# Weight scan with four load slots instead of two, and the first activation ladder on the vector engine alone: a two-layer Mamba and BitNet block on eight cores

## The reference, cut to what matters

```python
def act_quant(x):                     # per token, 8 bits
    scale = 127.0 / jnp.clip(jnp.max(jnp.abs(x), axis=-1, keepdims=True), EPS)
    return jnp.clip(jnp.round(x * scale), -128.0, 127.0) / scale
def weight_quant(w):                  # one scale for the whole matrix
    scale = jnp.clip(jnp.mean(jnp.abs(w)), EPS)
    return jnp.clip(jnp.round(w / scale), -1.0, 1.0) * scale
def h_bitlinear(x, w):
    return einsum(act_quant(fwht(x)), weight_quant(w))      # fwht: Hadamard rotation
x = x + mamba_and_ffn(layernorm(x))
y = layernorm(x)
x = x + h_bitlinear(silu(h_bitlinear(y, w_gate)) * h_bitlinear(y, w_up), w_down)
```

## Time and profile before

| what | value |
|---|---|
| median of three timed runs | 9508.48 us |
| lowest and highest of the three | 9263.67 and 9608.37 us |
| the profiled execution's own time | 9270.68 us |
| span of its slowest core (core 0) | 9269.1 us |
| spans of the eight cores | 9202.2 to 9269.1 us |
| granted TensorE clock, mean of each core | 0.767 to 0.769 |
| vector engine busy | 4310.0 us (46%) |
| TensorE matmuls busy | 4426.5 us (48%) |
| data moved by DMA on that core | 724.60 MB |

### The profile page before, as it was taken

The page is one execution under the profiler, slowest core; times in us unless marked ns, Lnnn a source line. Parts: engine busy times, 40 slices in busy tenths (PEclk is TensorE's granted clock), DMA queues, the critical chain, the costliest instruction groups (busy, mean ns, idle before and its releaser), DMA issues.

```text
span 9269.1 us, 76271 instructions; the slowest of 8 cores (9202.2 to 9269.1 us)
## 1 busy us (share of the span) xinstructions
PE 4426.5 (48%) x19532; PEld 1986.7 (21%) x19854; DVE 4310.0 (46%) x5807; ACT 1545.5 (17%) x2319; POOL 863.9 (9%) x859
## 2 busy tenths in 40 slices
PE   0002324854444365889889550688873000322247
PEld 0000111332332122334334120233330000110112
DVE  2222532443333331000000268677777888666678
ACT  2222231211101210000000013111110333121210
POOL 0000000000000000000000013100000343222210
PEclk9999657965555688999999775899985555666679
DMA  7764213310000033333333100344431000222247
GB/s 252 254 246 157 58 21 78 59 17 4 4 3 4 0 73 82 60 61 70 61 60 68 50 1 0 120 145 148 146 120 50 28 0 3 80 62 82 62 124 217
DMA packets 208574, 724.60 MB, mean 78 GB/s; under 512 B 49137, under 2 KB 50066, under 8 KB 179474
## 3 DMA queue, kind: packets, MB, share of 16 engines
q1 hardware_dynamic: 81890, 361.01, 11.7%
q0 software_dynamic: 68336, 205.28, 11.2%
q10 hardware_dynamic: 57920, 153.40, 5.4%
HBM read 817.63 MB, written 33.55 MB: 92 GB/s over the span
## 4 chain that ended last, share of the span: by engine, by line
PE 34%; DVE 33%; ACT 8%; DMA 8%; issue 8%; POOLq 5%; DVEq 3%; ACTq 2%; SPq 0%
PE pb L1087 10%; PE pb L1526 5%; PE pb L1132 5%; POOLq L85 5%; DVE arena L1199 4%; PE pb L365 3%; DVE arena L1696 3%; DVE arena L1210 2%; DVE arena L1405 2%; ACT arena L1187 2%; DMA arena<-fdT 2%; DMA arena<-fuT 2%; DMA arena<-fgT 2%; PE pb L789 2%; DVE arena L1692 2%
## 5 line engine op out<-in xcount | busy, mean ns | idle before, releaser
L1087 PE MATMUL pb<-arena 128*128 128x512 bf16 x4014 | 906.0, 381 | 330.3 <-DVE arena L1099 208.2
L1526 PE MATMUL pb<-arena 128*128 128x512 bf16 x4014 | 899.8, 380 | 119.5 <-DVE arena L1564 103.1
L1187 ACT ACTIVATE arena<-arena,c_ladthr 128x512 f32<-128x512 f32 x800 | 577.4, 722 | 2021.1 <-POOL arena L1222 1975.2
L1199 DVE SCALAR_TENSOR_TENSOR arena<-arena 128x512 f32<-128x512 f32 x800 | 705.7, 882 | 371.2 <-ACT arena L1187 306.1
L1222 POOL TENSOR_TENSOR arena<-arena 128x512 f32<-128x512 f32 x480 | 660.0, 1375 | 2088.5 <-DVE arena L1210 2032.9
L365 PE MATMUL pb<-arena 128*128 128x512 bf16 (+1 forms) x2853 | 506.8, 328 | 216.3 <-DMA arena<-winT 139.0
L1784 PE MATMUL pb<-arena 128*128 128x512 bf16 x2004 | 502.7, 405 | 202.6 <-DVE arena L1696 119.0
L1099 DVE TENSOR_TENSOR arena<-arena,pb 128x512 bf16<-128x512 bf16 x128 | 87.9, 687 | 1059.7 <-ACT arena L1094 1059.7
L1087 PEld LDWEIGHTS pb<-arena 128*128 128x128 bf16 x4096 | 393.3, 98 | 844.1 <-issue 394.6
L1526 PEld LDWEIGHTS pb<-arena 128*128 128x128 bf16 x4096 | 393.0, 98 | 627.3 <-issue 172.6
L1405 DVE TENSOR_REDUCE arena<-arena 128x1 f32<-128x2048 f32 x96 | 219.5, 2286 | 588.1 <-DMA arena<-fgT 197.3
(11 more groups left out here) (206 smaller groups left out, 5370.6 us busy)
## 6 DMA issues: line engine op xcount, KB each, us to landing
arena<-fdT ACTq DMA_DIRECT2D x256, 512.0 KB, 4.6
arena<-fgT SPq DMA_DIRECT2D x64, 1024.0 KB, 5.7
arena<-fuT SPq DMA_DIRECT2D x64, 1024.0 KB, 6.1
arena<-fdT SPq DMA_DIRECT2D x64, 1024.0 KB, 6.2
arena<-fgT SPq DMA_DIRECT2D x128, 512.0 KB, 4.2
arena<-fuT POOLq DMA_DIRECT2D x128, 512.0 KB, 4.2
arena<-wgT POOLq DMA_DIRECT2D x64, 512.0 KB, 5.0
arena<-wuT POOLq DMA_DIRECT2D x64, 512.0 KB, 5.0
```

Source lines behind the costliest of these rows:

```text
L1087: e.matmul(p[:, 0:nns], w[:, jj * 128:(jj + 1) * 128], self.rms2[:, jj * T + nn0:jj * T + nn0 + nns], start=st, stop=sp),
L1187: e.activation(cc[:], ss[:], AF.Sign, bias=self.ladthr[:, 16 + jj:17 + jj]),
L1199: e.scalar_tensor_tensor(ww[:], cc[:], -0.5 * kk, ss[:], OP.mult, OP.add),
L1526: e.matmul(pp[:, 0:nns], t2[:, jj * 128:(jj + 1) * 128], xq[:, jj * T + nn0:jj * T + nn0 + nns], start=st, stop=sp),
```

## The change

Three edits. In p0 the scan gets four slots instead of two: four buffers of 128 x 2048 float32, four semaphores (`p0x0` to `p0x3`), four loads ahead, and the load of tile j+4 is issued behind the sum of tile j. The split of the sums over the two engines stays. In p5 the ladder is no longer `ladder2_pair` on four tiles of 512 columns but `ladder` on one tile of 128 x 1024 after another, entirely on the vector engine. And `ln2` stays allocated until the end of p5 instead of being freed before the ladder; this alone issues no instruction and removes no barrier.

```diff
     def p5(self, stk, sC, sXQ):
-        sLN2 = ExitStack()
-        ln2 = self.sb(sLN2, [128, 16 * T], BF16, "ln2")
+        ln2 = self.sb(stk, [128, 16 * T], BF16, "ln2")
...
         Ss.barrier()
-        sLN2.close()
...
-        lbufs = [tuple(self.sb(stk, [128, 512], F32) for _ in range(3))
-                 for _ in range(4)]
-        for c in range(0, 16, 2):
-            tiles = [(c, 0), (c, 1), (c + 1, 0), (c + 1, 1)]
-            self.ladder2_pair(
...
-                lbufs, [("v", 0)] * 4)
+        v0 = self.sb(stk, [128, T], F32)
+        vt = self.sb(stk, [128, T], F32)
+        ct = self.sb(stk, [128, T], F32)
+        for c in range(16):
+            self.ladder(Y1[:, c * T:(c + 1) * T], scbc[:, 0:T], 0, T,
+                        xq[:, c * T:(c + 1) * T], v0, vt, ct, from_psum=False)
         Ss.barrier()

     def p0(self, stk):
-        wt_ = [self.sb(stk, [128, 2048], F32) for _ in range(2)]
+        wt_ = [self.sb(stk, [128, 2048], F32) for _ in range(4)]
...
-        st2 = Stream2(self, "sync", "p0x")
-        st2.load(0, wt_[0][:], srcs[0])
-        st2.load(1, wt_[1][:], srcs[1])
-        vprev, aprev = 0, 0
+        st2 = Stream2(self, "sync", "p0x", nslots=4)
+        for s4 in range(4):
+            st2.load(s4, wt_[s4][:], srcs[s4])
         for j, src in enumerate(srcs):
             if j % 2 == 0:
-                st2.wait("scalar", 0)
+                st2.wait("scalar", j % 4)
...
             else:
-                st2.wait("vector", 1)
+                st2.wait("vector", j % 4)
...
-            if j + 2 < len(srcs):
-                st2.load(j % 2, wt_[j % 2][:], srcs[j + 2],
-                         guard=(("a", aprev) if j % 2 == 0 else ("v", vprev)))
+            if j + 4 < len(srcs):
+                st2.load(j % 4, wt_[j % 4][:], srcs[j + 4], guard=tok)
```

More of the change, by code:

```diff
@@ L1391, in p0 @@
                 srcs.append(self.hbm["fdT"][m, :, q4 * 2048:(q4 + 1) * 2048])
-        st2 = Stream2(self, "sync", "p0x")
-        st2.load(0, wt_[0][:], srcs[0])
-        st2.load(1, wt_[1][:], srcs[1])
-        vprev, aprev = 0, 0
+        st2 = Stream2(self, "sync", "p0x", nslots=4)
+        for s4 in range(4):
+            st2.load(s4, wt_[s4][:], srcs[s4])
         for j, src in enumerate(srcs):
             if j % 2 == 0:
-                st2.wait("scalar", 0)
-                aprev = Ss.emit("scalar", lambda e, b=wt_[j % 2], jj=j:
-                                e.activation(dummy[:], b[:], AF.Abs,
-                                             accum_out=col[:, jj:jj + 1]), inc="a")
-            else:
-                st2.wait("vector", 1)
[L1404 to L1407, removed]
-            if j + 2 < len(srcs):
-                st2.load(j % 2, wt_[j % 2][:], srcs[j + 2],
-                         guard=(("a", aprev) if j % 2 == 0 else ("v", vprev)))
+                st2.wait("scalar", j % 4)
+                tok = ("a", Ss.emit(
+                    "scalar", lambda e, b=wt_[j % 4], jj=j:
+                    e.activation(dummy[:], b[:], AF.Abs,
+                                 accum_out=col[:, jj:jj + 1]), inc="a"))
+            else:
+                st2.wait("vector", j % 4)
+                tok = ("v", Ss.emit(
+                    "vector", lambda e, b=wt_[j % 4], jj=j:
+                    e.reduce_sum(col[:, jj:jj + 1], b[:],
+                                 axis=mybir.AxisListType.X,
+                                 apply_absolute_value=True), inc="v"))
+            if j + 4 < len(srcs):
+                st2.load(j % 4, wt_[j % 4][:], srcs[j + 4], guard=tok)
         Ss.barrier()
```

## The result

| | before | after |
|---|---|---|
| profiled execution | 9270.68 us | 9087.77 us |
| median of ten timed runs | 9458.35 us | 9201.34 us |
| lowest and highest | 9263.67 and 9672.41 us | 9081.15 and 9504.13 us |
| ratio of the two kernels' comparable runs | | 0.9818, 95% interval 0.9748 to 0.9889 |

The kernel became faster, by 1.1 to 2.5%; whether by more than 2% is not settled by these runs. Predicted were 9065 us (8980 to 9270) against the profiled execution, 2.2% less.

The account below looks back on a forecast made before the run. The prediction took p0 to be bound by the turn of its two load slots, and the ladder by a chain over three engines. It summed 9270.7 - 217 - 5 + 7 = 9056, said 9065 us, range 8980 to 9270.

Parts of the forecast that it names:

- The bound of p0: In p0, the turn of a slot (8.30 us, two side by side) limits the scan; more outstanding loads fill the missing 0.28.
- The rate: In p0 with four slots, DMA was taken to deliver 348 GB/s, so p0 takes 585.5 us, a gain of 217 us.
- if the time of a packet stays as it is: In p0, the assumption that scales a share of 0.73 at 256 GB/s to 351 GB/s at full share.
- the first rival: In p0, packets get longer with all cores asking; at 300 GB/s gain 125 us, kernel 9148 us; chance 0.28.
- the short stretches of 401 and 430: Full DMA stretches in p0, read as bounds from above; at 401 GB/s gain 293 us, kernel 8980 us, chance 0.10.
- those of 218 to 227: First 34 us of p0, kept for the deep-queues rival: p0 912 us, 109 more, kernel 9382 us; chance 0.04.
- Which core counts: At p0's end near 585 to 590 us, core 4 gains about 182, core 0 217; spans 9054 and 9052 us.
- The ladder: In p5, 16 tiles at 20.5 us make 328 us against 333.7, a gain of about 5 us.
- ln2 and the barriers: ln2 issues nothing; two more semaphores lengthen later barriers by 0.083 us a wait, at most 12 us, taken as 7.
- The level: Whole kernel: sum 9056 us, rounded up to 9065 us, predicted against the profiled execution of 9270.7 us.
- not reached by anything in its trace: Whole kernel: reason given for setting aside the 9508 us median of three timed runs, 238 above the profiled execution.
- The chance of 0.60 for more than 2%: Whole kernel: chance of gaining more than 2%, here 185 us, which needs a rate above about 331 GB/s in p0.

Follow-up runs that it names:

- Experiments 3 and 4: Changed kernel with three and with eight load slots in p0 instead of four: scan ends at 628 to 636 us and at 608 to 612 us.
- experiment 5: Changed kernel, scan copying one SBUF tile instead of weights from memory, weight means left out: 419 GB/s, last sums start at 491.8 to 493.8 us.
- experiment 2: Kernel before with only the new p5 ladder and the longer-lived ln2: ratio to the kernel before 1.0013 (0.9978 to 1.0048).
- experiment 8: Changed kernel with the scan's four semaphores left out of every later barrier: median span over the cores 9057.4 us, middle (stage1 to p4) 4489.3 us.
- experiments 6 and 7: Changed kernel with barriers leaving out already-done waits: profiled 8970.86 us; changed kernel with ten more already-reached waits in each barrier: profiled 9130.68 us.
- experiment 9: Changed kernel, p5's ladder replaced by multiply and add-and-take-away 12582912, two instructions per tile: profiled execution 8895.69 us, core 4 span 8779.6 us.
- experiment 4: Changed kernel with eight load slots in p0 instead of four: scan ends at 608 to 612 us, middle (stage1 to p4) 4499.8 us.

## Why the prediction was right or wrong

**The bound of p0: right.** The slot "stays empty from the start of its load to its landing": with four slots the DMA share is 1.00, the load takes 10.1 us (expected 11 to 12) and both sum engines wait for DMA as before. Experiments 3 and 4 show that the number of slots is no longer what counts.

**The rate: mis-sized by 3.5%.** I took 348 GB/s from the share of 0.73 at 256 GB/s. It is 336. The step that failed is "if the time of a packet stays as it is", taken from core 0 alone: cores 4 and 5 of the same trace had a share of 0.79 at 266 GB/s, which scales to 337. A share of 0.73 is not 0.27 of spare rate, since an engine that waits for memory counts as busy, and experiment 5 has 419 GB/s at the same share of 1.0. The scan gained 193 us on core 0, not 217. The mechanism of the first rival (packets get longer with all cores asking) was at work on core 0, at a quarter of the size that it had there (12 GB/s below 348, where the rival had 48), and cores 4 and 5 show none of it; the short stretches of 401 and 430 GB/s were no rate that can be held, and those of 218 to 227 no sign of harm.

**Which core counts: right.** All cores end p0 within 611 to 617 us; cores 4 to 7, which had been 34 to 43 us earlier than core 0, gained less, and the spans lie within 36 us.

**The ladder: right to a microsecond.** 328 us forecast, 328.3 measured, a gain of 5 forecast and 4.6 to 5.4 measured on core 0, alone (experiment 2) as well as together. The table of the Trainium skill, VectorE: DVE Perf Modes (The TRN2 errata), 58 cycles plus columns over the speed-up, would have given 290 as an estimate; its instructions take 1.225 and 0.753 us as the rows said.

**ln2 and the barriers: right in kind.** 7 us forecast, at most 12; the middle grew by 10.3 in the median of the cores, of which the price of a wait explains 6.7 (experiment 8). The 0.083 us a wait, read from one rest, is 0.07 by experiments 6 and 7.

**The level: wrong.** The sum gave 9056 and I said 9065 "against the profiled execution", whose counterpart came at 9087.8, a gain of 183 instead of 206. As the time of the changed kernel this number fits only its best executions: the median of ten is 9201, and against the median of before it would mean 4.2% where the comparison shows 1.8% (1.1 to 2.5). The step that failed is the dismissal of the 9508 as "not reached by anything in its trace", which put the distance between the median and the profiled execution at nothing. Two of the three timed runs shown were 238 us and more above the profiled one; in ten runs the median lies 188 us above it before (9458) and 114 after (9201). That spread belongs to both kernels, as the runs of after show (9081 to 9504), and a single traced execution can't show how often it comes. The direction held, and so did the 2.2% as a ratio, which lies inside the interval. The chance of 0.60 for more than 2% can't be judged by this: the rate passed the 331 GB/s that it asked for by 3 to 5, yet the profiled gain is 183 us, on the line of 2%, and the interval reaches to both sides of it.

## What to carry to other kernels

Give a streaming loop slots until the DMA share is 1.0 and stop there: the third slot brought most of it here and the fifth to eighth together 1 to 5 us. The spare share of a loop with too few slots can overstate the rate that memory will give, and it differs from core to core (336 to 351 GB/s here), so read it on all of them; here the lowest was the one that held. When work is moved from three engines to one at equal time, look first whether the work is needed: two instructions for a tile did in some 32 us (328 less the 296 that experiment 9 gave back) what 19 did in 328. And count what a generous barrier costs; 1684 waits that could never block took 117 us.

## What the runs showed of the hardware that I had not expected

A wait on a semaphore that has long been reached costs about 0.07 us: 51 us for 700 added and 117 us for 1684 removed. The counts are those of the vector engine; all engines were changed alike, so which of them the price falls on was not taken apart. Four semaphores more in experiment 4 did not show this price. A full DMA share hides which side is the bound: 336 GB/s from memory and 419 GB/s from SBUF both read as 1.0. And a float32 add of 12582912 with its subtraction in one tensor-scalar instruction does the ladder's rounding in 427 ns for 128 x 512, where a tensor-scalar of line 1210 takes 486; how it treats values halfway between two whole numbers was not examined.
